# Attention stage of a fused four-layer kernel: normalisations and key halves issued later, and value products of two units together

## What is computed

```python
def _L0_attn_ref(x, W_attn, b_attn, W_proj, b_proj):
    qkv = x @ W_attn + b_attn
    q, k, v = jnp.split(qkv, 3, axis=2)          # each to [B, 16 heads, T, 16]
    q = _rope_as_in_source(q)
    k = _rope_as_in_source(k)
    att = jnp.einsum('bhqd,bhkd->bhqk', q, k) * (1.0 / math.sqrt(hd))
    att = jnp.where(causal[None, None, :, :], att, -jnp.inf)
    att = jax.nn.softmax(att, axis=-1)
    y = jnp.einsum('bhqk,bhkd->bhqd', att, v)
    return y.transpose(0, 2, 1, 3).reshape(B, T, C) @ W_proj + b_proj
```

## Time and profile before

| what | value |
|---|---|
| median of 3 runs | 3524.84 us (3515.46 to 3532.96) |
| profiled execution, its own time | 3520.16 us |
| its span, first to last instruction | 3518.2 us |
| mean granted TensorE clock | 0.909 of full speed |
| PE, DVE, ACT, POOL busy share of the span | 82%, 54%, 36%, 20% |
| first and last `exp` matmul of the attention stage | 116.8 us and 1489 us |

### The profile page before, as it was taken

How to read it: one execution, slowest core, us unless ns; L and a number is a source line. 1 busy time by engine, 2 the same in 40 slices (tenths; PEclk the granted TensorE clock), 3 DMA queues, 4 the chain that set the end, 5 groups by cost and what they waited for, 6 DMA issues and landing times. The chain is left out here.

```text
span 3518.2 us, 44483 instructions
## 1 busy us (share of the span) xinstructions
PE 2899.9 (82%) x15561; PEld 1776.5 (50%) x15561; DVE 1912.7 (54%) x5455; ACT 1262.4 (36%) x2117; POOL 714.6 (20%) x1101
## 2 busy tenths in 40 slices
PE   3899898989898989823788886579898989989876
PEld 1344343434343434322677765455665656566554
DVE  2766666657575757564566565444525344353442
ACT  1465555555555555621222220113132131322311
POOL 5031414140404040110112112011302112020211
PEclk8799999999999999966988897789999999999998
DMA  4241414141424232131322222200101001010000
GB/s 127 59 128 44 151 44 151 44 151 44 137 58 121 74 109 74 38 118 43 104 72 97 84 96 72 79 18 22 51 0 51 21 30 51 0 51 12 12 24 12
DMA packets 172169, 235.41 MB, mean 67 GB/s; under 512 B 17117, under 2 KB 138873, under 8 KB 165762
## 3 DMA queue, kind: packets, MB, share of 16 engines
q1 hardware_dynamic: 172002, 233.27, 21.6%
HBM read 131.74 MB, written 101.50 MB: 66 GB/s over the span
## 5 line engine op out<-in xcount | busy, mean ns | idle before, releaser
L942 ACT ACTIVATE pt<-ps 128x1024 f32<-128x1024 f32 (+3 forms) x768 | 601.0, 811 | 336.0 <-PE ps L857 225.0
L769 DVE CUSTOM_DVE_ANT_0 masked<-ps,mask_q 128x128 bf16<-128x128 f32 (+3 forms) x1024 | 473.8, 484 | 279.3 <-PE ps L835 275.5
L835 PE MATMUL ps<-sk,sq 96*128 96x512 bf16 (+3 forms) x1536 | 442.1, 346 | 80.6 <-DMA sk<-scratch_stacks 27.6
L854 PE MATMUL ps<-sq,sk 99*128 99x512 bf16 (+3 forms) x1536 | 416.6, 339 | 63.8 <-DMA sq<-scratch_nm_parts 33.2
L773 DVE TENSOR_REDUCE mx<-ps 128x1 f32<-128x512 f32 x512 | 351.8, 687 | 156.8 <-PE ps L835 156.3
L835 PEld LDWEIGHTS ps<-sk,sq 96*128 96x128 bf16 x1536 | 136.9, 99 | 411.5 <-issue 125.6
L873 PE MATMUL ps<-pt,val 128*32 128x512 f32 (+3 forms) x3072 | 334.3, 508 | 1.1 <-ACT yt L950 0.9
L854 PEld LDWEIGHTS ps<-sq,sk 99*128 99x128 bf16 x1536 | 152.6, 101 | 209.3 <-ACT pt L942 76.5
L1948 PE MATMUL ps<-eht,w_fc 128*128 128x512 f32 x512 | 249.7, 636 | 9.5 <-ACT eht L1999 9.5
L1960 PE MATMUL ps<-w_fc,eyb 128*128 128x256 f32 x1024 | 228.7, 381 | 15.5 <-ACT eyb L2007 15.5
L1960 PEld LDWEIGHTS ps<-w_fc,eyb 128*128 128x128 f32 x1024 | 193.3, 190 | 53.7 <-ACT eyb L2007 24.5
(11 more groups left out here) (294 smaller groups left out, 4866.8 us busy)
## 6 DMA issues: line engine op xcount, KB each, us to landing
scratch_stacks<-part SPq DMA_DIRECT2D x32, 768.0 KB, 3.6
sq<-scratch_stacks SPq DMA_DIRECT2D x32, 768.0 KB, 7.9
sk<-scratch_stacks SPq DMA_DIRECT2D x32, 768.0 KB, 9.1
scratch_stacks<-part SPq DMA_DIRECT2D x32, 512.0 KB, 4.5
x<-in_L_attn_x SPq DMA_DIRECT2D x8, 1024.0 KB, 14.3
scratch_stacks<-part SPq DMA_DIRECT2D x32, 256.0 KB, 4.9
xr<-in_L_attn_x SPq DMA_DIRECT2D x8, 1024.0 KB, 6.1
scratch_x<-xr SPq DMA_DIRECT2D x8, 1024.0 KB, 10.3
```

Source lines behind the costliest of these rows:

```text
L769: nc.vector.tensor_tensor_reduce(mem["masked"][:, slot, 0:n], ps[:, RING[slot], 0:n], mem["mask_q"][:, BANK - n:BANK], 1.0, -3e38, ALU.add ...
L835: nc.tensor.matmul(ps[:, bank, 0:n], sq[0:ROWS, h, i * P:(i + 1) * P], sk[0:ROWS, h, half * BANK:half * BANK + n], start=True, stop=True)\
L854: last = nc.tensor.matmul(ps[:, bank, 0:n], sk[0:ROWS_M, h, j * P:(j + 1) * P], sq[0:ROWS_M, h, q0:q0 + n], start=True, stop=not diag)
L942: nc.scalar.activation(pt[:, u % 3, 2 * pair:2 * pair + 2, 0:n], ps[:, bank:bank + 2, 0:n], ACT.Exp, scale=SCALE).then_inc(e["exp_done"], 1)
```

## The change

It alters `attention_steps` alone; no engine code changes, so every instruction stays and only the order changes.

```diff
-                put(before + 9 + t, *[("x_norm", b, j) for j in tiles[2 * t:2 * t + 2]])
-            put(before + 13, ("xt", b, 0, 0), ("xt", b, 0, 1))
-            put(before + 14, ("xt", b, 1, 0), ("xt", b, 1, 1))
+                put(before + 11 + t, *[("x_norm", b, j) for j in tiles[2 * t:2 * t + 2]])
+            put(before + 14, ("xt", b, 0, 0), ("xt", b, 0, 1))
+            put(before + 15, ("xt", b, 1, 0), ("xt", b, 1, 1))
...
-                put(at + 4, ("parts", b, 1, chunk, 0))
-                put(at + 5, ("parts", b, 1, chunk, 1))
+                put(at + 6, ("parts", b, 1, chunk, 0))
+                put(at + 7, ("parts", b, 1, chunk, 1))
...
-            put(behind + 19 + t, *[("a_norm", b, j) for j in tiles[2 * t:2 * t + 2]])
-            put(behind + 22 + t, *[("x1_stat", b, j) for j in tiles[2 * t:2 * t + 2]])
+            put(behind + 21 + t, *[("a_norm", b, j) for j in tiles[2 * t:2 * t + 2]])
+            put(behind + 24 + t, *[("x1_stat", b, j) for j in tiles[2 * t:2 * t + 2]])
...
-        if 0 < t <= turn * B:
-            b, (s, g) = (t - 1) // turn, divmod((t - 1) % turn, n_eu)
-            order.append(("av", b, s, g))
-            if g == n_eu - 1 or EU[g + 1][0] != EU[g][0]:
-                order.append(("y_out", b, s, EU[g][0]))
+        if 0 < t <= turn * B and t % 2 == 0:
+            for u in (t - 2, t - 1):
+                b, (s, g) = u // turn, divmod(u % turn, n_eu)
+                order.append(("av", b, s, g))
+                if g == n_eu - 1 or EU[g + 1][0] != EU[g][0]:
+                    order.append(("y_out", b, s, EU[g][0]))
```

## The result

The changed kernel takes 3496.65 us (median of 6 runs, 3486.62 to 3504.12), the kernel before 3526.51 us in the same series (6 runs, 3515.46 to 3532.96). The ratio is 0.9918, with a 95% interval of 0.9896 to 0.9941: faster by 30 us. The forecast was 3442 us with a range of 3396 to 3490, so the sign was right, and 55 us of the expected gain are missing; the time lies above the range.

What follows compares the result with a forecast made beforehand. PE's own list was taken to bound the attention stage, leaving its idle time and low clock to win. Gains of 33 + 47 + 0 = 80 us from 3520.2 gave 3440, stated as 3442 us for the median; range 3396 to 3490.

Steps and rivals of the forecast that it cites:

- the three holes: PE idle in steps 10, 23 and 35 of a batch, costing 5.3, 8.2 and 6.5 us with the lower clock.
- the charge of 0.6 us a batch for the neighbours: Steps 13 to 15: ACT normalisations of the moved xt lie nearer its copies and exponentials; bounds 0 and 1.1 us.
- Tail: Steps 21 to 24, a_norm and k halves two units later: 7.8 us per batch, 47 us in six.
- rival B: Steps 21 to 25: clock drop returns or k halves hold up ACT; 26 us less gain, 3468 us; chance 0.17.
- Value blocks in pairs: PE's value blocks two per even step: 0.21 us saved per pair, offset by three prices; net nil.
- the third: Price of pairing at DVE: ring banks hold 1.8 us against a 2.0 us double block; 1.2 us a batch.
- The copy of the maxima: Price of pairing: `rows` at odd steps loses the block covering its ACT copy, steps 33 and 45; 0.9 us a batch.
- ACT's exponentials: Price of pairing: second `exp` waits about 0.3 us in steps 8, 20, 32 and 44; 1.3 us a batch.
- rival A: Pairing value blocks earns all of its 0.21 us per pair: 3404 us; chance 0.17.
- D: The moves do less since the next wait lies right behind: 20 us in all, 3500 us; chance 0.07.
- C: Slower: the double block empties both consumers, DVE and ACT; 0.54 us net per pair, 104 us, 3546 us; chance 0.07.

Runs made afterwards that it cites:

- moves alone: The changed kernel with value blocks issued one unit at every step, as in the kernel before, instead of in pairs: 3427.26 us, ratio 0.9734 to the kernel before.
- Head: The kernel before with only x_norm two steps later and xt one step later: 3483.13 us, ratio 0.9880.
- tail alone: The kernel before with only the k halves, a_norm and x1_stat two steps later: 3471.02 us, ratio 0.9857.

## Why the prediction came out wrong

**What bounds the kernel, and the three holes: right.** The moves alone gained 87 us in the stage and 98 us timed, against a forecast of 80. Head: forecast 33 us between 30 and 37, measured 42. In steps 9 to 16, which the move touches, it is 37 us: the hole and its low clock are gone whole, and the charge of 0.6 us a batch for the neighbours didn't come. The other 5 us lie in steps that the move doesn't touch (0, 23, 24 and 35) and are not explained. Tail: 47 between 21 and 50, measured 50 in the stage and 54 timed. With the tail alone, step 24 begins 9.0 us after step 21 (mean of batches 1 to 6; forecast 8.8, before 13.9), and steps 24 and 25, now at full clock, take 3.1 us less (forecast 3.2). That is 8.0 us a batch, 48 us in six batches, close to the 5.0 + 3.2 = 8.2 that the prediction worked out and then took as 7.8 without a reason. The wait for the copy in step 21 is short there, and in the moves alone as well:

```profile
PE ps L835 <- ACT nmr L975: 5.5, 7, 0.8
```

(waits view of the moves alone).

**Steps 21 to 24 of the changed kernel: right in order, and the clock wrong.** The wait in step 21 is 1.99 us where I had some 2, POOL splits at once, and the next `nm`, at step 36, is not late (3.3 us in all). Where the clock stays up (batch 1), step 24 begins at 8.75 us, forecast 8.8. But I had argued that only holes of 3.5 us and more go with a drop, and the clock falls in 6 of the 7 batches with this wait: in five of them behind the wait of 1.99 us alone, which makes step 24 1.6 us later (10.35 against 8.75), and in batch 3 behind the waits of 1.99 and 0.99 us, where steps 24 and 25 take 13.5 instead of 12.2 us. That was the first half of rival B, and it costs 1.3 to 1.6 us a batch of the 4.3 that I gave it. From step 21 to step 26 the changed kernel saves 6.7 us a batch and the tail alone 8.0.

**Value blocks in pairs: the step that failed.** I had "35 won to 28 lost" and took nil; measured, pairs cost 69 us timed and 61 in the stage beside the moves, and 55 and 63 without them. The saving of 0.21 us per pair was right in size (0.24 measured in the double block), though I let only 15 of 24 pairs earn it. The prices failed, the third above all:

- "The three ring banks hold about 3 x 0.6 = 1.8 us" and "In quiet steps DVE has a third of its time free and is not hurt", charged at 1.2 us a batch. The waits of `max` for DVE rose from 16.2 us in the moves alone to 59.0 us, 5.3 us a batch. I looked at the gap in DVE's supply during the even step, and averaged over the pair. What matters is the burst in the odd step: four or five maxima in a row against three banks. DVE's free third doesn't help there, as it lies in the double block, before the maxima are there. The cost is PE's, not DVE's: about half of the block that used to cover it.
- The copy of the maxima: 0.9 us a batch, for steps 33 and 45 alone. The waits went from 5.5 to 19.0 us, 1.7 us a batch. Steps 33 and 45 took only 0.55 of it, less than I charged; 1.1 are in step 21, whose 2 us the prediction had seen, but in the tail's paragraph and without a price.
- ACT's exponentials: 1.3 us a batch. The waits rose by only 2.3 us in all; this price was too high.

The rises in these three (42.8 + 13.5 + 2.3) less 4.2 us for the reloaded maxima make 54 of the 61 us in the stage. This is idle time alone; with the 46 us of fixed cost saved, the whole loss is about 107 us, 13 us a batch, where the prediction had charged 3.4.

**Sums.** Some of the working doesn't add up. 3440.2 + 4.7 is 3445, not 3442; rival A is worth 38 us in one place and 40 in another; and the tail's lower bound "without the clock gain" is 3.5 us a batch where the same paragraph has 5.0 saved without it. The range holds the bounds of each term one at a time. All three lower bounds at once (30 + 21 - 28 = 23 us) would be 3502, so the measured time lay inside the bounds of the terms and outside the stated range; that is no merit, as the moves came in at the top and the pairs far below.

**Rivals.** The time is near that of D (3500), but D's reason is wrong: the moves did more than they said, not less. C comes nearest, as it has the two consumers of PSUM in it and a loss per pair: measured 69 / 192 = 0.36 us net. But C starves them by the length of the double block, and that is not what costs. With no double block anywhere, the kernel with the block behind the last third loses twice as much. The burst that follows is in no rival. The Trainium skill's warning, that once TensorE is tiled emptying PSUM may be the limit (TensorEngine Tiling (Array Packing), PSUM Bottleneck), holds here in an odd form: DVE is busy only 65% of the stage, and PE waits for it 59 us, since the limit is a burst against three banks at one place in the order and not DVE's mean rate. I gave C 0.07 because I read its chance from DVE's share of busy time. My range didn't hold the time since for pairs its lower bound stopped at 28 us lost.

**What stays open.** The parts outside the stage have the same code in all kernels, and take 2139 to 2157 us from one profile to another; so single profiles don't settle 10 us, and why pairs cost 69 us timed (65 by the ratios) beside the moves but 55 without them is not known. It is not in the stage. Why the clock falls behind the same wait in six batches and not in batch 1 is open too.

## What to carry to other kernels

Before taking an instruction out of a place in an in-order list, ask what it covers there: a wait that no view shows, as the instruction fills it, appears when it goes. Test a burst against the number of buffers in that one step, not the mean rate over two. And when small operations of one engine are moved for the sake of another, check on which side of that engine's next urgent duty they land.

## What the runs showed of the hardware

A value block of 32-column tiles between bf16 matmuls of full height costs 0.24 us beyond its passes: 0.10 us going in and 0.13 to 0.15 us coming out (the earlier trace rows and step 42 above). Coming out it is 0.14 us at all four widths from 128 to 512 columns, with 8 matmuls in the block or 16. The Trainium skill says that a change of the tiling mode drains the engine (TensorEngine Tiling (Array Packing), Key Properties). A fixed cost at both ends agrees with that; the traces can't show that it is a drain.

The granted clock fell to 0.50, the lower of its two levels (1.2 instead of 2.4 GHz), behind a single wait of 1.99 us in five batches, and behind waits of 1.99 and 0.99 us with 6.7 us of work in 9.9 us in one. In one batch with the same wait of 1.99 us it stayed at 1.00. In the moves alone, where PE's wait for the copy in step 21 is 0.8 us, it fell in steps 21 to 24 of no batch, though PE also waits 0.4 to 1.4 us at step 24 there.
